# A gated cross-attention layer on one core: the second tile's input prepared during the weight folds, two input tiles turned earlier, and the second tile's probabilities turned in pieces

## The chip, the cores and the metric

The kernel runs on one core of one Trainium2 chip. The metric is the device time of one execution in microseconds. The version before the change took 1050.38 us (median of three runs, 1048.02 to 1050.64).

## The reference, cut to what matters

```python
q, k, v = split_heads(ln(x) @ Wq), split_heads(ctx @ Wk), split_heads(ctx @ Wv)   # 16 heads of 64
attn = softmax(q @ k.T * 64 ** -0.5)
x = x + tanh(g_xattn) * (merge_heads(attn @ v) @ Wo + bo)       # x is 4 x 2048 x 512, ctx is 4 x 77 x 384
idx = argmax(log_softmax(logits) + gumbel(u))                   # one of 8 weight matrices
x = x + tanh(g_ffn) * (ln(x) @ W[idx] + b[idx])
```

`ln` is a layer norm without weights, `merge_heads` puts the heads side by side.

## The kernel before, in words

**Folds.** The context is small (4 batches of 77 keys), so the program first folds weights into it. For each batch and head, Wq times the keys gives one matrix against which a normalized x is multiplied directly, and the values times Wo give one matrix by which the probabilities are multiplied. The folds are the visits of the list `VISITS`: 16 value visits (`VALUE`, PE line L1502), 32 key visits (`KEY`, PE L1510) and some others, on four pairs of PSUM banks in turn. Each fold is copied to float16 as a high part by ACT (L842 for values, L855 for keys) and as the remaining low part by DVE (L1098, L1109). For some folds ACT only stages a float32 copy (L840, L853), and POOL splits it (L681 and L683, L691 and L693). The next fold on a pair of banks waits until the fold four visits earlier has been taken. The value visits 13, 14 and 15 stand among the key visits 18 to 24; key visits 24 to 31 come last.

**Tiles.** Then x is worked off in 64 tiles of 128 rows, numbered 0 to 63; tile m is row block m // 4 of batch m % 4. A tile goes through these stages:

- `load_x` (SP, L497) brings tiles m+2 and m+3 at even m. `x_moments` (DVE, L1038) and `x_variance` (L1042), `x_scale` (POOL, L649 to L654), `x_normalized` and `x_high` (ACT, L792 and L799) and `x_low` (DVE, L450) make the normalized x as a high and a low float16 part in the stage `xs`. `turn_x` (SP, L487) transposes `xs` by a DMA.
- `scores` (PE, L1397, 36 matmuls) fills three of four PSUM banks. `maxima` (DVE, L1190, L1192), `exponentials` (ACT, 16 times L890), `softmax` (DVE, L1199, L1201), `probs_high` (ACT, L905, L907) and `probs_low` (DVE, L450) make the probabilities in two float16 parts in the one buffer `ps`. ACT's copy L990 fills its tail.
- SP turns `ps` into `pT` by a DMA transpose of 20 blocks (L589). There is one `pT`, so SP first waits for the semaphore `o_done`, which tells that the attention of the tile before is finished. For tiles 0 and 63 (`turned_early`) it goes in four pieces: 6 blocks of the high part and 6 of the low part (L582), which need the first 12 heads only, then 4 blocks (L586) and 4 blocks (L589).
- `attention` (PE, 27 matmuls of L1397 and two of L1625; in pieces L1608 to L1618) multiplies the turned probabilities by the folded values, and `attention_sum` (DVE, L1219) adds x.
- Two tiles later the feed-forward matrix is applied to a pair of tiles by seven products of half the size (Strassen's scheme; PE L1397 with 256 columns), with their stages turned by SP (L501, groups 0 to 3) and added by DVE (L1277). The seven weight combinations are made once, in the steps of tiles 0 to 2, by POOL (`weights_summed`), ACT (`weights_high`, L957) and DVE (`weights_low`, L1295) from a second load of the matrix (SP, L521).

**What sets the order.** Every engine runs `step` once a tile, and each engine's order within a step is written out by hand. The engines wait for each other by semaphores alone, and every engine, SP too, works in order: an instruction that waits holds all behind it. Step m computes scores of tile m and attention of tile m-1 on PE. DVE and ACT make the normalized x of tile m+1 in step m, and DVE takes the moments of tile m+2 there. Steps 0 to 5 are unrolled, steps 6 to 61 are seven turns of a loop of eight steps, and the last ones are unrolled again.

**Around the change.** Before the steps, tile 0 is made ready amid the folds: its moments at `(PROJECT, 3)`, its ACT part at `(VALUE, 2)` and `(REMAINDER, 3)`. Tile 1 has its moments at `(KEY, 24)`, and its ACT and DVE parts at the head of step 0, behind the last fold. On SP the transposes for tiles 0 and 1 stand behind waits for the folds:

```python
sp.wait_ge(v_folded, 4 * VALUES)
sp.dma_start(xr[:, 1, :], x[1, 0:P, :]).then_inc(x_loaded[1], 16)
sp.wait_ge(bo_set, 16 * 2 * B)
turn_x(0, 0)
sp.wait_ge(v_stage_lo, len(STAGED_VALUES))
sp.wait_ge(side_lo, 4 * KT)
sp.dma_start(wf_raw, ffn_w[...]).then_inc(wf_again, 16)
sp.wait_ge(k_stage_lo, key_staged_before(UNITS))
turn_x(0, 1)
```

`xr` has eight places for x tiles. Places 1 to 6 are under other data until the value folds are done; place 7 is free, apart from the turned x of tile 1, which stands there.

## Time and profile before

| | us |
|---|---|
| median of three runs | 1050.38 |
| the profiled execution's own time | 1049.61 |
| its span (first to last instruction) | 1047.8 |
| PE busy | 1029.6 (98% of the span) |
| DVE busy | 853.0 (81%) |
| ACT busy | 744.7 (71%) |
| POOL busy | 443.8 (42%) |
| PE's share of the chain that ended last | 91% |

PE's busy share counts every matmul from its start to its modelled end. The chain that ended last is followed back from the last instruction, at each step to what released it. Times in the tables of the trace count from the start of the span. The idle time before an instruction stands in brackets behind it, with what ended it.

### The profile page before, as it was taken

What the parts mean: (1) busy time and instruction counts of PE and PEld (TensorE: products, weight loads), DVE (VectorE), ACT (ScalarE), POOL (GpSimd) and SP (SyncE); (2) the same over time, 40 slices, a digit from 0 to 9 for tenths busy, and PEclk for the clock granted to TensorE, in tenths of its full rate; (3) what the DMA queues carried; (4) which work ended last, traced back from release to release, by engine and by line L of the source; (5) the groups of instructions that cost most, each with busy time, mean ns of one, the idle gap of its engine ahead of it and who ended that gap; (6) DMA issues with size and microseconds to landing.
All of it is one profiled execution on the core that took longest, in us unless ns stands there. A gap on an engine that the chain in (4) does not pass through costs nothing.

```text
span 1047.8 us, 21829 instructions
## 1 busy us (share of the span) xinstructions
PE 1029.6 (98%) x6065; PEld 588.2 (56%) x6065; DVE 853.0 (81%) x1802; ACT 744.7 (71%) x2712; POOL 443.8 (42%) x639
## 2 busy tenths in 40 slices
PE   8988899999999999999999999999999999999998
PEld 6634455555555555555555555555555555555555
DVE  4877988888888887888888887888888887888876
ACT  3588877767776777767776777767776777767762
POOL 1486443444333443444333443444333443444422
PEclk9999999999999999999999999999999999999999
DMA  8423476555666656655666656655666656655656
GB/s 307 99 37 98 94 127 141 126 112 119 135 138 138 136 126 133 134 114 115 133 139 138 136 125 134 134 115 114 133 139 138 137 123 135 136 114 114 133 113 141
DMA packets 383639, 135.02 MB, mean 129 GB/s; under 512 B 361728, under 2 KB 363316, under 8 KB 383540
## 3 DMA queue, kind: packets, MB, share of 16 engines
q1 hardware_dynamic: 383476, 134.09, 59.0%
q14 instruction: 84, 0.69, 0.2%
q8 instruction: 15, 0.25, 0.1%
q0 software_dynamic: 64, 0.00, 0.0%
HBM read 27.48 MB, written 16.78 MB: 42 GB/s over the span
## 4 chain that ended last, share of the span: by engine, by line
PE 91%; DVE 4%; DMA 2%; ACT 2%; issue 1%; SPq 0%; POOL 0%; DVEq 0%; ACTq 0%
PE banks L1397 82%; PE banks L1625 3%; PE banks L1427 1%; PE banks L1502 1%; PE banks L1438 1%; DMA work<-work 1%; ACT work L890 1%; PE banks L1510 1%; DMA fold_area<-in_L_xattn_Wv 1%; DVE work L450 1%; DVE vw_area L1098 1%; ACT vw_area L842 1%; PE banks L1491 1%; DVE fold_area L1109 0%; DVE work L1201 0%
## 5 line engine op out<-in xcount | busy, mean ns | idle before, releaser
L890 ACT ACTIVATE work<-banks,red,cst 128x77 f32<-128x77 f32 x1024 | 410.3, 431 | 83.9 <-DVE red L1192 83.4
L1397 PE MATMUL banks<-fold_area,work 128*128 128x456 f16 (+1 forms) x2304 | 405.4, 335 | 3.0 <-DMA work<-work 2.3
L1397 PE MATMUL banks<-vw_area,work 128*128 128x512 f16 x1674 | 373.1, 380 | 3.0 <-DMA work<-work 3.0
L1397 PEld LDWEIGHTS banks<-fold_area,work 128*128 128x128 f16 x2304 | 225.2, 98 | 171.6 <-DMA work<-work 3.1
L1397 PEld LDWEIGHTS banks<-vw_area,work 128*128 128x128 f16 x1674 | 164.0, 98 | 189.2 <-DMA work<-work 3.7
L450 DVE SCALAR_TENSOR_TENSOR work<-work 128x256 f16<-128x256 f32 (+3 forms) x443 | 240.9, 578 | 1.4 <-ACT work L799 0.6
L890 ACT ACTIVATION_READ_ACCUMULATOR work<-banks,red,cst 128x1 f32 x1024 | 224.8, 220 | 0.0
L1190 DVE TENSOR_REDUCE stats<-banks 128x6 f32<-128x462 f32 (+1 forms) x192 | 112.0, 583 | 103.9 <-PE banks L1397 103.7
L1397 PE MATMUL banks<-work 128*128 128x256 f16 x1302 | 162.4, 272 | 0.5 <-DVE work L1277 0.3
L1397 PEld LDWEIGHTS banks<-work 128*128 128x128 f16 x1302 | 126.8, 98 | 32.0 <-DVE work L1277 0.6
L734 POOL TENSOR_TENSOR stats<-stats,cst 128x1 f32<-128x1 f32 x64 | 12.5, 195 | 284.1 <-DVE stats L1226 284.1
L905 ACT ACTIVATE work<-work 128x768 f16<-128x768 f32 (+1 forms) x128 | 82.0, 640 | 58.6 <-DVE work L1201 58.6
L649 POOL TENSOR_TENSOR stats<-stats,cst 128x1 f32<-128x1 f32 x64 | 50.1, 783 | 169.4 <-DVE stats L1042 169.4
L792 ACT ACTIVATE work<-work,stats 128x512 f32<-128x512 f32 x64 | 52.1, 813 | 96.9 <-POOL stats L654 81.3
L1201 DVE TENSOR_TENSOR work<-work,cst 128x924 f32<-128x924 f32 (+1 forms) x128 | 113.5, 886 | 4.4
L1277 DVE SCALAR_TENSOR_TENSOR work<-banks,cst,work 128x256 f32<-128x256 f32 x217 | 97.9, 475 | 21.9 <-issue 18.2
L758 POOL TENSOR_TENSOR work<-work 128x512 f32<-128x512 f32 x64 | 95.9, 1499 | 43.0 <-DVE work L1235 33.5
L913 ACT ACTIVATE work<-work 128x512 f16<-128x512 f32 x123 | 71.1, 578 | 5.4 <-DMA work<-work 3.7
L1192 DVE TENSOR_SCALAR red<-stats,cst 128x6 f32<-128x6 f32 (+1 forms) x192 | 61.0, 318 | 6.8
L1219 DVE SCALAR_TENSOR_TENSOR work<-banks,cst,work 128x512 f32<-128x512 f32 x64 | 47.6, 744 | 6.8 <-PE banks L1625 3.6
L752 POOL TENSOR_TENSOR work<-work 128x256 f32<-128x256 f32 x31 | 45.2, 1459 | 2.4
L1222 DVE BATCH_NORM_STATS2 stats<-work 128x6 f32<-128x512 f32 x64 | 44.4, 694 | 2.2
(148 smaller groups left out, 819.4 us busy)
## 6 DMA issues: line engine op xcount, KB each, us to landing
work<-in_x SPq DMA_DIRECT2D x64, 256.0 KB, 2.8
out<-work SPq DMA_DIRECT2D x63, 256.0 KB, 2.2
work<-work SPq DMA_TRANSPOSE x253, 3.1
fold_area<-in_L_xattn_Wo SPq DMA_DIRECT2D x4, 512.0 KB, 9.6
work<-in_L_ffn_W SPq DMA_DIRECT2D x2, 1024.0 KB, 7.5
fold_area<-in_L_xattn_Wq SPq DMA_DIRECT2D x2, 1024.0 KB, 13.0
fold_area<-in_L_xattn_Wk SPq DMA_DIRECT2D x2, 768.0 KB, 12.4
fold_area<-in_L_xattn_Wv SPq DMA_DIRECT2D x2, 384.0 KB, 7.6
```

What stands on the lines that cost most here:

```text
L450: return nc.vector.scalar_tensor_tensor(out=lo, in0=value, scalar=scale, in1=hi, op0=ALU.mult, op1=ALU.subtract)
L649: nc.gpsimd.tensor_tensor(ve1, mv1[:, 1:2], eps, ALU.add).then_inc(ve1_ready, 1)
L758: nc.gpsimd.tensor_tensor(xr[:, m2, :], xr[:, m2, :], bias, ALU.add).then_inc(x2b_ready, 1)
L792: nc.scalar.activation(xn_place(o1, m1), xr[:, m1, :], ACT.Identity, bias=nm1, scale=rstd1).then_inc(xn_ready, 1)
L890: nc.scalar.activation(probs_of(place, place + 1), s_heads(m, k)[:, h - h0, :], ACT.Exp, bias=nmx[:, h:h + 1], scale=exp_scale, accum_out= ...
L905: nc.scalar.activation(by_core(ps[:, h0 * CORE:h1 * CORE]), values[:, :, 0:CORE], ACT.Copy, scale=2.0 ** PROB_BITS).then_inc(p_hi, 1)
L913: nc.scalar.activation(group_stage(g, last)[:, 0, :], value, ACT.Copy, scale=2.0 ** XN_BITS).then_inc(x2_hi, 1)
L1190: nc.vector.reduce_max(mx[:, h0:h1], s_heads(m, k), AX.X).then_inc(mx_ready, 1)
L1192: nc.vector.tensor_scalar(nmx[:, h0:h1], mx[:, h0:h1], nexp_scale, None, ALU.mult).then_inc(nmx_ready, 1)
L1201: nc.vector.tensor_tensor(values, values, factors.unsqueeze(2).to_broadcast([P, h1 - h0, J]), ALU.mult).then_inc(p_ready, 1)
L1277: nc.vector.scalar_tensor_tensor(out=half, in0=part, scalar=f_scale, in1=half, op0=ALU.mult, op1=ALU.add).then_inc(f_added, 1)
L1397: mm = nc.tensor.matmul(ps, lhs(l), rhs(r), start=first and n == 0, stop=last and n == 2, skip_group_check=onto)
```

## The change

1. **Tile 1's x during the folds.** A load of its own brings tile 1 into place 7 of `xr` (`x_second`) right behind tile 0's load. Its moments are taken at key visits 10 and 11, its scale at 14, its ACT parts at 20 and 21, and its low part at 22. The load into place 1 stays where it was, for `attention_sum`. SP turns tile 0 before it waits for the value folds, and tile 1 right behind that load, ahead of the second load of the feed-forward matrix.
2. **Tiles 2 and 3.** DVE makes their low part after two of the three maxima of steps 1 and 2, not after all three.
3. **Every even step on SP.** `turn_x` now stands ahead of the two loads of x, where it stood behind them.
4. **Tile 1's probabilities** are turned in the four pieces, and multiplied so. The load of the bias moves behind them.
5. Two semaphores of start-up constants become one.

```diff
--- before.py
+++ after.py
@@ -142,6 +142,7 @@
         bias = c.take(D)
         assert c.at == 16592
         ident = bias[:, 0:P]
+        x_second = xr[:, RING - 1, :]
         xT_second = xr[:, RING - 1, :].bitcast(F16).rearrange("p (s k n) -> p s k n", s=2, k=KT)
         pT_last = fold_area[:, 0:KEYS // 2].bitcast(F16).rearrange("p (c n) -> p c n", n=P)
 
@@ -322,7 +324,7 @@
         EARLY = BANKS[1][1] * CORE // P
 
         def turned_early(o, m):
-            return is_tile(o, m, 0, NT - 1)
+            return is_tile(o, m, 0, 1, NT - 1)
 
         def heads_of(piece):
             return BANKS[piece[0]][0], BANKS[piece[1] - 1][1]
@@ -473,6 +475,7 @@
                 rows = slice(n * KT // 2, (n + 1) * KT // 2)
                 sp.dma_start(wq_raw[:, rows, :], wq.rearrange("(k p) n -> p k n", p=P)[:, rows, :]).then_inc(wq_loaded[n], 16)
             sp.dma_start(xr[:, 0, :], x[0, 0:P, :]).then_inc(x_loaded[0], 16)
+            sp.dma_start(x_second, x[1, 0:P, :]).then_inc(x_second_loaded, 16)
 
             def due(semaphore, count):
 
@@ -512,15 +515,15 @@
                 for s in range(2):
                     sp.dma_start(vw_side[TAIL + TH:TAIL + TH + 1, :, b, 2 * s + 1, :],
                                  bo_split[0:1, s, :].rearrange("p (t n) -> p t n", t=KT)).then_inc(bo_set, 16)
+            sp.wait_ge(bo_set, 16 * 2 * B)
+            turn_x(0, 0)
             sp.wait_ge(v_folded, 4 * VALUES)
             sp.dma_start(xr[:, 1, :], x[1, 0:P, :]).then_inc(x_loaded[1], 16)
-            sp.wait_ge(bo_set, 16 * 2 * B)
-            turn_x(0, 0)
+            turn_x(0, 1)
             sp.wait_ge(v_stage_lo, len(STAGED_VALUES))
             sp.wait_ge(side_lo, 4 * KT)
             sp.dma_start(wf_raw, ffn_w[bass.ds(op, 1), :, :].rearrange("o (k p) n -> p (o k) n", p=P)).then_inc(wf_again, 16)
             sp.wait_ge(k_stage_lo, key_staged_before(UNITS))
-            turn_x(0, 1)
 
             def step(o, m):
                 o1, m1 = tile(o, m, 1)
@@ -536,12 +539,12 @@
                         if positive(*pair, 2):
                             due(f_done, nth_pair(*pair, PRODUCTS))
                         turn_group(2)
+                    if valid(o1) and not is_tile(o, m, 0):
+                        turn_x(o1, m1)
                     for lag in (2, 3):
                         ol, ml = tile(o, m, lag)
                         if valid(ol):
                             load_x(ol, ml)
-                    if valid(o1) and not is_tile(o, m, 0):
-                        turn_x(o1, m1)
                     if is_tile(o, m, NT):
                         turn_lone(NT - 2)
                     if valid(pair[0]) and paired(*pair):
@@ -571,10 +574,8 @@
                     early = turned_early(o, m)
                     if not positive(o, m, 1):
                         sp.wait_ge(pad_zeroed, 2)
-                    elif not early:
+                    elif not early or is_tile(o, m, 1):
                         due(o_done, nth(o, m))
-                    if is_tile(o, m, 1):
-                        sp.dma_start(bias, ffn_b[bass.ds(op, 1), :].to_broadcast([P, D])).then_inc(bias_loaded, 16)
                     if early:
 
                         for s, half_ready in enumerate((p_hi, p_lo)):
@@ -587,6 +588,8 @@
                     due(p_lo, nth(o, m, 4) + 4)
                     start = NC + EARLY if early else 0
                     sp.dma_start_transpose(turned[:, start:, :], ps[:, start * P:]).then_inc(pT_turned, 16)
+                    if is_tile(o, m, 1):
+                        sp.dma_start(bias, ffn_b[bass.ds(op, 1), :].to_broadcast([P, D])).then_inc(bias_loaded, 16)
                 if is_tile(o, m, NT):
                     store_pair(*tile(o, m, -6))
                 if is_tile(o, m, NT + 1):
@@ -701,7 +704,7 @@
                     key_split(n)
                 if (kind, n) == (REMAINDER, 1):
                     x_scale(0, 0)
-                if (kind, n) == (KEY, 24):
+                if (kind, n) == (KEY, 14):
                     x_scale(0, 1)
 
             pool.wait_ge(a_done, 2 * UNITS)
@@ -789,7 +792,7 @@
                 if not is_tile(o1, m1, 0, 1):
                     act.wait_ge(xT_turned, nth(o1, m1, 16))
                     act.wait_ge(p_lo, nth(o1, m1, 4) - 4)
-                nc.scalar.activation(xn_place(o1, m1), xr[:, m1, :], ACT.Identity, bias=nm1, scale=rstd1).then_inc(xn_ready, 1)
+                nc.scalar.activation(xn_place(o1, m1), x_second if is_tile(o1, m1, 1) else xr[:, m1, :], ACT.Identity, bias=nm1, scale=rstd1).then_inc(xn_ready, 1)
 
             def x_high(o1, m1):
 
@@ -876,6 +879,10 @@
                     x_normalized(0, 0)
                 if (kind, n) == (REMAINDER, 3):
                     x_high(0, 0)
+                if (kind, n) == (KEY, 20):
+                    x_normalized(0, 1)
+                if (kind, n) == (KEY, 21):
+                    x_high(0, 1)
             act.wait_ge(exp_scale_ready, 2)
 
             def exponentials(o, m, k):
@@ -898,9 +905,9 @@
                     act.wait_ge(pad_zeroed, 2)
                 elif n == 0:
                     act.wait_ge(pT_turned, nth(o, m, 16))
-                    if is_tile(o, m, 1):
+                    if is_tile(o, m, 1, 2):
                         for part_turned in pT_parts:
-                            act.wait_ge(part_turned, 16)
+                            act.wait_ge(part_turned, 16 * number(o, m))
                 values = by_head(probs_of(h0, h1))
                 nc.scalar.activation(by_core(ps[:, h0 * CORE:h1 * CORE]), values[:, :, 0:CORE], ACT.Copy,
                                      scale=2.0 ** PROB_BITS).then_inc(p_hi, 1)
@@ -962,7 +969,7 @@
                 grouped = valid(pair[0]) and paired(*pair)
                 if is_tile(o, m, NT + 1):
                     lone_high(NT - 1)
-                if valid(o1):
+                if valid(o1) and not is_tile(o, m, 0):
                     x_normalized(o1, m1)
                     x_high(o1, m1)
                 if grouped:
@@ -1034,8 +1041,11 @@
 
             def x_moments(o1, m1):
 
-                dve.wait_ge(x_loaded[m1], o1 * 16 + 16)
-                nc.vector.bn_stats(bn1, xr[:, m1, :]).then_inc(x_stats, 1)
+                if is_tile(o1, m1, 1):
+                    dve.wait_ge(x_second_loaded, 16)
+                else:
+                    dve.wait_ge(x_loaded[m1], o1 * 16 + 16)
+                nc.vector.bn_stats(bn1, x_second if is_tile(o1, m1, 1) else xr[:, m1, :]).then_inc(x_stats, 1)
 
             def x_variance():
 
@@ -1175,11 +1185,13 @@
                     x_low(0, 0)
                 if (kind, n) == (KEY, 12):
                     scales()
-                if (kind, n) == (KEY, 24):
+                if (kind, n) == (KEY, 10):
                     x_moments(0, 1)
-                if (kind, n) == (KEY, 25):
+                if (kind, n) == (KEY, 11):
                     dve.wait_ge(x_stats, 2)
                     x_variance()
+                if (kind, n) == (KEY, 22):
+                    x_low(0, 1)
 
             NB = len(BANKS)
 
@@ -1216,6 +1228,8 @@
                 dve.wait_ge(o_done, nth(o, m) + 1)
                 if not positive(o, m, 1):
                     dve.wait_ge(o_scale_ready, 2)
+                if is_tile(o, m, 1):
+                    dve.wait_ge(x_loaded[1], 16)
                 nc.vector.scalar_tensor_tensor(out=xr[:, m, :], in0=o_ps, scalar=o_scale, in1=xr[:, m, :],
                                                op0=ALU.mult, op1=ALU.add).then_inc(x2_ready, 1)
                 dve.wait_ge(x2_ready, nth(o, m) + 1)
@@ -1346,8 +1360,6 @@
                     added(*begun, 3)
                 if valid(o2):
                     dve.wait_ge(x2_stats, nth(o2, m2) + 1)
-                if is_tile(o, m, 0):
-                    x_low(o1, m1)
                 if valid(o):
                     maxima(o, m, 0)
                 if grouped:
@@ -1356,11 +1368,13 @@
                     x2_variance(o2, m2)
                 if valid(o):
                     maxima(o, m, 1)
+                if is_tile(o, m, 1, 2):
+                    x_low(o1, m1)
                 if valid(o2):
                     x2_normalized(o2, m2)
                 if valid(o):
                     maxima(o, m, 2)
-                if valid(o1) and not is_tile(o, m, 0):
+                if valid(o1) and not is_tile(o, m, 0, 1, 2):
                     x_low(o1, m1)
                 if is_tile(o, m, 1):
                     weights_low(AS_LOADED, 0)
@@ -1584,7 +1598,7 @@
             def attention(o, m):
 
                 b, turned, early = m % B, probs_place(o, m), turned_early(o, m)
-                turns = 16 if is_tile(o, m, 0) else 32
+                turns = 16 if is_tile(o, m, 0) else 32 if is_tile(o, m, 1) else 48
                 if early:
                     pe.wait_ge(pT_parts[0], turns)
                 else:```

The order of the instructions on ACT, at the end of the folds and the head of step 0, was this (`vw_area` and `fold_area` hold the folded values and keys; L840 and L853 are staged copies, L792 and L799 tile 1's normalized x and its high part, L957 the weights):

```order
L842 CAST vw_area<-banks 128x1024
L855 CAST fold_area<-banks 128x4x76x2
L840 COPY work<-banks 128x1024
L855 CAST fold_area<-banks 128x4x76x2
L842 CAST vw_area<-banks 128x1024
L855 CAST fold_area<-banks 128x4x76x2
L853 COPY work<-banks 128x608
L855 CAST fold_area<-banks 128x4x76x2 x6
L853 COPY work<-banks 128x608
L855 CAST fold_area<-banks 128x4x76x2
L792 ACTIVATE work<-work,stats 128x512
L799 ACTIVATE work<-work 128x512
```

With the change it is this (lines are three higher):

```order
L845 CAST vw_area<-banks 128x1024
L858 CAST fold_area<-banks 128x4x76x2
L795 ACTIVATE work<-work,stats 128x512
L843 COPY work<-banks 128x1024
L858 CAST fold_area<-banks 128x4x76x2
L802 ACTIVATE work<-work 128x512
L845 CAST vw_area<-banks 128x1024
L858 CAST fold_area<-banks 128x4x76x2
L856 COPY work<-banks 128x608
L858 CAST fold_area<-banks 128x4x76x2 x6
L856 COPY work<-banks 128x608
L858 CAST fold_area<-banks 128x4x76x2
```

The two instructions of tile 1 moved from behind the last key fold to either side of value visit 14, ahead of 11 of its copies.

SP's queue from the bias rows to tile 1's probabilities was this (`[waits ...]` names the semaphores waited for):

```order
L513 DMA vw_area<-work 1x4x128 x7
L516 DMA work<-in_x 128x512 [waits v_folded]
L487 DMA_TRANSPOSE work<-work 128x8x128 [waits bo_set,x_lo]
L521 DMA work<-in_L_ffn_W 128x4x512 [waits side_lo,v_stage_lo]
L487 DMA_TRANSPOSE work<-work 128x8x128 [waits k_stage_lo,x_lo]
L497 DMA work<-in_x 128x512 x2
```

It is now:

```order
L516 DMA vw_area<-work 1x4x128 x7
L490 DMA_TRANSPOSE work<-work 128x8x128 [waits bo_set,x_lo]
L521 DMA work<-in_x 128x512 [waits v_folded]
L490 DMA_TRANSPOSE work<-work 128x8x128 [waits x_lo]
L525 DMA work<-in_L_ffn_W 128x4x512 [waits side_lo,v_stage_lo]
L500 DMA work<-in_x 128x512 [waits k_stage_lo]
```

Both transposes of x (L487, now L490) moved ahead by one transfer each; the matrix's second load stands behind the second.

SP's queue of an even step, number 4, was this (L501 turns groups of the feed-forward, L589 the probabilities):

```order
L501 DMA_TRANSPOSE work<-work 128x8x128 [waits x2_lo]
L497 DMA work<-in_x 128x512
L497 DMA work<-in_x 128x512 [waits xT_turned]
L487 DMA_TRANSPOSE work<-work 128x8x128 [waits x_lo,s_done]
L501 DMA_TRANSPOSE work<-work 128x4x128 [waits x2_lo]
L589 DMA_TRANSPOSE work<-work 128x20x128 [waits o_done,p_tail,p_lo]
```

And now:

```order
L504 DMA_TRANSPOSE work<-work 128x8x128 [waits x2_lo]
L490 DMA_TRANSPOSE work<-work 128x8x128 [waits x_lo,s_done]
L500 DMA work<-in_x 128x512
L500 DMA work<-in_x 128x512 [waits xT_turned]
L504 DMA_TRANSPOSE work<-work 128x4x128 [waits x2_lo]
L590 DMA_TRANSPOSE work<-work 128x20x128 [waits o_done,p_tail,p_lo]
```

The two loads stand behind the waits of the transpose of x.

## Rows read from the trace of the kernel before

**Rows 1.** Waits of PE from 91 to 143 us: total, times, longest.

```profile
PE banks L1397 <- DMA work<-work: 5.3, 4, 2.6
```

**Rows 2.** PE in order of time: start us, duration us, what, idle before.

```profile
91.56 6.33 PE L1397 MATMUL banks<-fold_area,work 128*128 128x456 f16 x36 [0.77 <-ACT work L853]
99.36 6.34 PE L1397 MATMUL banks<-fold_area,work 128*128 128x456 f16 x36 [1.47 <-DMA work<-work]
...
121.75 7.69 PE L1397 MATMUL banks<-vw_area,work 128*128 128x512 f16 x27 [2.64 <-DMA work<-work]
...
136.42 6.00 PE L1397 MATMUL banks<-vw_area,work 128*128 128x512 f16 x27 [0.38 <-DMA work<-work]
```

**Rows 3.** Busy time by stretch; PEclk is the granted share of TensorE's clock.

```profile
121.75:125.10 3.35, 3.35 (x9) 1.21 (x10) 3.21 (x7) 3.35 (x17) 0.00 (x0) 0.52 0.76 212
```

**Rows 4.** The chain that ended last, 129 to 137 us: start us, us, what.

```profile
129.44 0.45 PE banks L1625 x2
...
130.56 5.81 DMA work<-work
```

**Rows 5.** ACT in order of time, the last folds and the head of step 0.

```profile
80.77 0.70 ACT L855 CAST fold_area<-banks 128x608 f16<-128x608 f32 x1
81.59 1.01 ACT L840 COPY work<-banks 128x1024 f32<-128x1024 f32 x1
...
83.42 1.01 ACT L842 CAST vw_area<-banks 128x1024 f16<-128x1024 f32 x1 [0.21 <-PE banks L1502]
...
91.43 0.82 ACT L792 ACTIVATE work<-work,stats 128x512 f32<-128x512 f32 x1
92.28 0.63 ACT L799 ACTIVATE work<-work 128x512 f16<-128x512 f32 x1
92.81 1.32 ACT L957 ACTIVATE work<-work,red 128x512 f16<-128x512 f32 x2
...
95.16 0.42 ACT L890 ACTIVATE work<-banks,red,cst 128x77 f32<-128x77 f32 x1 [1.03 <-DVE red L1192]
```

**Rows 6.** DVE in order of time.

```profile
69.46 1.23 DVE L1098 TENSOR_TENSOR vw_area<-banks,vw_area 128x1024 f16<-128x1024 f32 x1 [1.17 <-ACT vw_area L842]
...
87.06 0.68 DVE L1038 BATCH_NORM_STATS2 stats<-work 128x6 f32<-128x512 f32 x1
...
92.94 1.37 DVE L450 SCALAR_TENSOR_TENSOR work<-work 128x512 f16<-128x512 f32 x1 [0.58 <-ACT work L799]
...
127.74 1.67 DVE L450 SCALAR_TENSOR_TENSOR work<-work 128x768 f16<-128x768 f32 x4
```

**Rows 7.** POOL in order of time.

```profile
85.40 2.13 POOL L683 TENSOR_TENSOR vw_area<-work,vw_area 128x1024 f16<-128x1024 f32 x1
...
92.10 1.65 POOL L693 TENSOR_TENSOR fold_area<-work,fold_area 128x608 f16<-128x608 f32 x1
```

**Rows 8.** SP's issues in order of time.

```profile
87.56 0.41 SPq L521 DMA_DIRECT2D work<-in_L_ffn_W  x1
94.41 1.25 SPq L487 DMA_TRANSPOSE work<-work  x1
```

**Rows 9.** Line L521 from 87 to 88 us.

```profile
DMA to landing us min/median/max: 5.1/5.1/5.1
```

**Rows 10.** SP's issues in step 8 and step 14.

```profile
209.96 1.23 SPq L487 DMA_TRANSPOSE work<-work  x1
...
305.56 3.01 SPq L589 DMA_TRANSPOSE work<-work  x1
```

**Rows 11.** Line L497, the two loads of x from 207 to 209 us.

```profile
DMA to landing us min/median/max: 2.6/2.7/2.7
```

**Rows 12.** DVE in step 8.

```profile
212.27 0.69 DVE L1038 BATCH_NORM_STATS2 stats<-work 128x6 f32<-128x512 f32 x1
```

**Rows 13.** Line L589, the 58 transposes of probabilities from 150 to 1000 us.

```profile
DMA to landing us min/median/max: 4.9/4.9/6.5
```

**Rows 14.** PE, attention of tile 14.

```profile
312.48 0.81 PE L1397 MATMUL banks<-vw_area,work 128*128 128x512 f16 x3
```

13 lines of the change are left out of this document (7 added, 6 removed).

## The prediction

> **What bounds the kernel now.** I read the page first: PE is busy 98% of the span and 91% of the chain that ended last, so there is little to win, and only where PE stands still. The waits of PE show where: from 91 to 143 us it waits 5.3 us for transposes, four times [rows 1], and after that hardly at all until the tail. PE in order of time gives the places [rows 2]: 1.47 us before the scores of tile 1, 2.64 before the attention of tile 1, 0.38 before the attention of tile 2, which leaves 0.80 for the scores of tile 2. There is a second loss behind the longest wait: the 27 matmuls at 121.75 take 7.69 us, and the same 27 at 136.42 take 6.00 [rows 2]. The granted clock in the first 3.35 us of the slow ones is 0.52 [rows 3], mostly the lower of the two levels (1.2 instead of 2.4 GHz). The engine had been idle for 2.64 us before it, while the wait of 1.47 us left the clock alone. So all that this change can reach is 5.3 + 1.69 = 7.0 us, plus what it does to the folds.
>
> The question is then what sets the last of these waits, because behind it PE runs through: the total moves by as much as the end of tile 2's attention moves. The chain says that its transpose at 130.56 was released by PE itself, by the end of tile 1's attention (129.44 + 0.45) [rows 4], since the buffer is shared. But DVE's low parts of tile 2's probabilities end only at 127.74 + 1.67 = 129.41 [rows 6]. If PE comes earlier, the transpose can start at 129.5 at the earliest, 1.1 us sooner, unless DVE and ACT come earlier too. That is the step on which I rest.
>
> **The change part by part.** I count against the profiled execution (1049.61 us, 0.77 below the median of the runs, 1050.38).
>
> *Tile 1's moments.* DVE's 0.68 us at key visits 10 and 11 fall into an idle 1.17 us before 69.46 [rows 6]: nothing. POOL's scale lies ahead of a split that has no one waiting; it moves POOL by under 1 us and is made up by its removal at visit 25. The load of its own (256 KB behind tile 0's) has over 40 us: nothing.
>
> *ACT amid the folds.* Its two instructions take 0.82 + 0.63 = 1.45 us [rows 5]. Idle time that can take them is 81.59 - (80.77 + 0.70) = 0.12 and 0.21 us [rows 5], so the copy of value visit 15, at 83.42, comes up to 1.1 us later, and all key visits behind it are in its tow.
>
> *DVE amid the folds.* The low part stands, within one key fold, where the moments' 0.68 us stood at 87.06 [rows 6]. It is the same tile of work, but in the trace it took 1.37 us at 92.94 [rows 6], while POOL's subtraction ran from 92.10 to 93.75 [rows 7]; it ended 0.56 us after that. In its new place POOL's longer subtraction (2.13 us at 85.40 before [rows 7]) is running. Bounds: equal to the moments (0) and 1.37 - 0.68 = 0.7 more; I take 0.7, since that row is of the same instruction beside the same kind of work. The Trainium skill (SBUF — State Buffer, "SBUF: two separate sides") says that a VectorE operation with two SBUF inputs and a GpSimd operation that reads SBUF lock a port pair for a whole instruction and block each other fully. The trace agrees (0.56 us after POOL's end). By that rule alone the worst case is 2.13 + 0.56 = 2.7 us, and the sum would be 1.3 us higher than mine; the sum goes by the row.
>
> Together: ACT's delay of up to 1.1 partly hides in DVE's waits for ACT, the 0.7 adds up. The scores of tile 0, released by the last staged copy at 91.56 [rows 2], start 0.3 (all but a remainder hidden) to 1.8 us (both in full) later; I take 1.3.
>
> *Start of tile 0's exponentials*, now at 95.16 [rows 5]. Two things hold them. Through the scores: 1.3 later, less 0.3 that DVE's low part of tile 1 had cost there (it ended at 94.31 [rows 6], the first bank, 12 of the 36 matmuls, at about 91.56 + 2.4), so 96.2. Through SP: the second load of the matrix, issued at 87.56 [rows 8], now stands behind the transpose of tile 1, which waits for the low part (87.06 + 1.37 = 88.4) and takes 1.25 us to issue [rows 8], so it goes out at 89.8. It lands 5.1 us later [rows 9], plus some 0.3 for sharing the DMA engines with that transpose: 95.2. ACT's two weight copies, 1.32 us [rows 5], wait for it and stand ahead of the exponentials: 96.5. The later one counts: **the chain of tile 0 starts 1.4 us later** (0.3 to 2.2), although tile 1's x is ready early. What the folds gain PE, namely the wait of 1.47 us, only turns up again as a wait of about 1.7 us before tile 0's attention, whose first pieces come 1.4 us later.
>
> *From there to tile 2.* ACT and DVE are back to back from these exponentials to DVE's end at 129.41, and nothing in between is removed. Tile 2's and 3's low parts only change places with a maximum (0 to 0.3, if POOL's sums hit them; 0). So tile 2's probabilities are ready at 129.41 + 1.4 = 130.8.
>
> *Tile 1's pieces.* SP now issues the first 6 blocks while the last heads' low parts are still made, about 2 us before the whole transpose could have gone, and PE needs the rest only 2.6 us after its start. The attention of tile 1 follows the scores of tile 2 without a wait: 2.64 and the 1.69 us of slow clock are gone there. PE then comes to tile 2's attention at about 92.85 + 4 x 6.2 (scores) + 2 x 6.4 (attention) + 1.7 (wait) = 132.2.
>
> *Tile 2's attention* is not turned in pieces. Issued at 130.9, landed 5.81 us later [rows 4], it starts at 136.75 instead of 136.42: **+0.3**. Landing in 4.9 us, the usual value [rows 13], would make it -0.6. PE has then stood still for some 4.5 us, longer than the 2.64 us that were followed by the low clock, so I let the slow stretch come back here, once: the 27 matmuls take 7.69 again, **+1.7**. With no slow stretch the bound is 0.
>
> *Loads behind `turn_x`.* In each even step the two loads now wait for the transpose of x. In step 8 it is issued at 209.96 [rows 10], so the load goes at about 211.3 and lands at 213.9 with 2.6 to 2.7 us [rows 11]. DVE takes that tile's moments at 212.27 [rows 12]: a new wait of 1.65 us on DVE, with the last softmax and the low parts queued behind it. PE waits for these through the transpose. In the tightest even step, 14 (the first of each turn of the loop), it is issued at 305.56 [rows 10], lands after 4.9 [rows 13], and PE takes it at 312.48 [rows 14]: 2.0 us of slack, of which 0.4 are left. So it costs nothing as long as landings stay at 4.9; the cover is that slack.
>
> Sum: +0.3 + 1.7 + 0 = +2.0 us on 1049.61, or 1050.38 + 2.0 = **1052.4** for the median. That is 0.19%; about 0.3% (3.15 us) is what a measurement of this kernel can tell from no change, so it reads as no difference.
>
> **The rivals.** *A, the wait moves and the clock holds.* The low clock followed one idle stretch in this part of the trace, and one case is thin ground. With it gone, or with a landing of 4.9 us, the sum is -0.6 to +0.6; with the chain only 0.3 late it is -1.7: 1048.7 to 1051.0, say 1050.4.
>
> *B, slower: the loop's slack breaks.* One of the 58 transposes took 6.5 us to land [rows 13], so landings do vary. If the loads' 1.65 us exceed what the first even step of each loop turn has left, PE stops there: with half a microsecond in each of seven turns, 3.5 us on top of 2.0, so 1055.9. It decides from 0.4 us of lateness on. Against it: the median landing is also the least, 4.9 us [rows 13].
>
> *C, faster: PE's gain is kept.* If the chain of waits is right that PE's own end released tile 2's transpose, and ACT and DVE come earlier with it, 5.3 + 1.69 less 0.4 for tile 2 is won: 1050.38 - 6.6 = 1043.8. Against it: the 129.41 of rows 6 would have to become 125 or so, and the folds' end moves the other way.
>
> **How the numbers follow.** Forecast 0.62, A 0.14, B 0.16, C 0.08. The forecast's own bounds run from 1050.5 (chain 0.4 late, clock low) to 1053.2 (chain 2.2 late). For the range I go down over A's middle and up to most of B: 1049.0 to 1055.5; outside are C, the top of B and the bottom of A. Faster by over 0.3% is C (0.08); slower by over 0.3% is B and a little of the forecast's top (0.18); the rest is 0.74.
>
> **What would show it.** Right if: PE has no wait between the scores of tiles 0 and 1, waits 1 to 2.5 us before tile 0's attention, none before tile 1's and 4 to 5 us before tile 2's; 7.7 us instead of 6.0 in tile 2's attention and 6.0 in tile 1's; L957's first copies start at about 95 us; DVE waits 1.5 to 1.8 us for a load in every even step. Wrong if tile 2's transpose is issued before 129.5 us, if the exponentials of tile 0 start at 95.2 or before, or if PE waits in the loop.

## The result, and the profile after

| | before | after |
|---|---|---|
| median of 20 runs each, on one chip | 1048.10 us | 1052.56 us |
| ratio, 95% interval | | 1.0044 [1.0032, 1.0056] |
| the profiled execution, its own time / span | 1049.61 / 1047.8 us | 1058.05 / 1056.2 us |

The change costs 0.44%, some 4.6 us: slower by more than the 0.3% that can be told from no change. The forecast was 1052.4, +2.0 us on a median of 1050.38. That the time came within 0.2 us of the forecast is luck: the kernel before ran at 1048.1 this time, 2.3 us faster than the median that I had counted from, and of the difference the forecast had less than half. The interval leaves out two disturbed runs of after (2793.52 and 3848.48 us); the others lie between 1048.36 and 1058.05, and the profiled one is the slowest of them. Its rows show mechanisms, and their sizes have to be averaged over runs.

PE of after in order of time, to be read against [rows 2]. L1411 is what L1397 was, L1622 begins an attention in pieces.

```profile
93.99 12.50 PE L1411 MATMUL banks<-fold_area,work 128*128 128x456 f16 x72 [0.77 <-ACT work L856]
108.02 2.76 PE L1622 MATMUL banks<-vw_area,work 128*128 128x512 f16 x12 [1.53 <-DMA work<-work]
...
120.46 2.75 PE L1622 MATMUL banks<-vw_area,work 128*128 128x512 f16 x12
...
128.47 6.34 PE L1411 MATMUL banks<-fold_area,work 128*128 128x456 f16 x36 [1.59 <-DMA work<-work]
138.06 8.94 PE L1411 MATMUL banks<-vw_area,work 128*128 128x512 f16 x27 [3.25 <-DMA work<-work]
```

The 72 matmuls at 93.99 are the scores of tiles 0 and 1 without a wait. Tile 0's attention waits 1.53 us, tile 1's not at all, the scores of tile 3 wait 1.59, tile 2's attention 3.25, and its 27 matmuls take 8.94 us. The windows of PE there (us, PE busy, PEclk, DMA share, GB/s), against [rows 3]:

```profile
138.06:143.00 4.94, 4.94 (x12) 0.50 0.35 66
143.00:146.80 3.80, 3.80 (x16) 0.86 0.37 69
```

The clock stood at its lower level (1.2 of 2.4 GHz) for 6.8 us in all (0.85 us of it still in the pause), twice as long as in before.

ACT of after amid the last folds and at the head of step 0, against [rows 5]:

```profile
82.49 0.83 ACT L795 ACTIVATE work<-work,stats 128x512 f32<-128x512 f32 x1
84.67 0.66 ACT L802 ACTIVATE work<-work 128x512 f16<-128x512 f32 x1
85.20 1.03 ACT L845 CAST vw_area<-banks 128x1024 f16<-128x1024 f32 x1
96.48 1.33 ACT L964 ACTIVATE work<-work,red 128x512 f16<-128x512 f32 x2 [2.53 <-DMA work<-in_L_ffn_W]
97.72 0.40 ACT L897 ACTIVATE work<-banks,red,cst 128x77 f32<-128x77 f32 x1
```

DVE's low part of tile 1, against [rows 6], and POOL's subtraction beside it, against [rows 7]:

```profile
88.10 1.37 DVE L452 SCALAR_TENSOR_TENSOR work<-work 128x512 f16<-128x512 f32 x1
```

```profile
86.80 2.13 POOL L686 TENSOR_TENSOR vw_area<-work,vw_area 128x1024 f16<-128x1024 f32 x1
```

DVE's instruction took 1.37 us again and ended 89.47 - 88.93 = 0.54 us after POOL's, as it had ended 0.56 after it in before; the matrix's load landed at 96.38, and ACT's weight copies and the exponentials stood behind it. The chain that ended last (start us, us, what) holds the transfers, against [rows 4, 9]:

```profile
91.03 5.35 DMA work<-in_L_ffn_W
...
96.48 1.33 ACT work L964 x2
...
132.55 5.46 DMA work<-work
...
138.06 2.31 PE banks L1411 x5
```

The start of the program differs between executions. So I count from the start of tile 0's moments on DVE (42.45 us in before, 43.60 in after). From there:

| start of | before | after | difference | forecast |
|---|---|---|---|---|
| scores of tile 0 | 49.11 | 50.39 | +1.28 | +1.3 |
| exponentials of tile 0 | 52.71 | 54.12 | +1.41 | +1.4 |
| attention of tile 2 | 93.97 | 94.46 | +0.49 | +0.3 |
| attention of tile 4 | 122.77 | 126.21 | +3.44 | +2.0 |
| attention of tile 61 | 961.80 | 969.03 | +7.23 | +2.0 |

The first three lines came as forecast. The fourth is 1.4 us above its forecast, nearly all of it in tile 2's attention, which took 8.94 us and not 7.69. The last line holds 3.79 us that are lost between tile 4 and tile 61, where I had put nothing. The waits from 150 to 1010 us show where (total, times, longest), DVE's and then PE's:

```profile
DVE stats L1048 <- DMA work<-in_x: 53.5, 29, 3.6
```

```profile
PE banks L1411 <- DMA work<-work: 2.5, 3, 1.0
```

29 waits of DVE for a load, 1.84 us each, were forecast (1.65). In before DVE waits for no load in this stretch and PE for no transpose. One of PE's three waits, and how it came about, told by the chain that ended last:

```profile
319.21 6.00 PE L1411 MATMUL banks<-vw_area,work 128*128 128x512 f16 x27 [0.85 <-DMA work<-work]
```

```profile
306.87 1.23 SPq L490
...
308.41 2.52 DMA work<-in_x
...
310.95 0.71 DVE stats L1048
...
313.31 0.78 DVE work L452 x3
...
314.19 4.90 DMA work<-work
...
319.21 2.98 PE banks L1411 x13
```

The transpose of x goes first, then the load, then DVE's moments, the last softmax and low parts, then the transpose of tile 14's probabilities, then PE. All transfers have their usual length here, and PE still waited 0.85 us. The slack of 2.0 us that I read from [rows 10, 13, 14] was more than gone: the transpose was issued 319.21 - 0.85 - 314.19 = 4.17 us before PE was ready for it, where it had been 6.92 in before. That is 2.75 us later, not the 1.65 that I had counted.

One thing in the waits of before bears on why the first even step of a turn is the tightest, and my account had left it out. Six times, at the start of a turn, DVE stands still for some 3 us, for which the profile shows no releaser. What it does in that time is not shown. The line gives the total, the times and the longest:

```profile
DVE work L1277 <- issue: 18.2, 6, 3.1
```

### The profile page after: what moved, and what is told of

It reads as the page before. It is cut to its first block, busy times and chain, and to the rows that moved or that the text cites. A ratio compares the mean times of both kernels' runs of the same rounds, so it can differ in the third digit from the quotient of the medians.

```text
span 1056.2 us, 21836 instructions
## 1 busy us (share of the span) xinstructions
PE 1033.6 (98%) x6065; PEld 589.3 (56%) x6065; DVE 854.1 (81%) x1802; ACT 740.0 (70%) x2712; POOL 443.5 (42%) x639
## 4 chain that ended last, share of the span: by engine, by line
PE 75%; DVE 8%; DMA 5%; issue 4%; ACT 3%; POOL 2%; SPq 2%; DVEq 0%; ACTq 0%; POOLq 0%
PE banks L1411 67%; DVE work L452 3%; PE banks L1639 2%; ACT work L897 2%; DMA work<-in_x 2%; DMA work<-work 1%; PE banks L1441 1%; PE banks L1452 1%; PE banks L1516 1%; SPq L490 1%; DVE stats L1202 1%; DVE stats L1048 1%; ACT vw_area L845 1%; DMA fold_area<-in_ctx 1%; DVE vw_area L1108 1%
## 5 line engine op out<-in xcount | busy, mean ns | idle before, releaser
L897 ACT ACTIVATE work<-banks,red,cst 128x77 f32<-128x77 f32 x1024 | 409.7, 428 | 35.8 <-DVE red L1204 35.8
L1411 PE MATMUL banks<-fold_area,work 128*128 128x456 f16 (+1 forms) x2304 | 405.2, 335 | 2.4 <-DMA work<-work 1.6
L1411 PE MATMUL banks<-vw_area,work 128*128 128x512 f16 x1647 | 368.4, 381 | 5.8 <-DMA work<-work 5.8
L1411 PEld LDWEIGHTS banks<-fold_area,work 128*128 128x128 f16 x2304 | 225.3, 98 | 170.6 <-DMA work<-work 2.1
L1411 PEld LDWEIGHTS banks<-vw_area,work 128*128 128x128 f16 x1647 | 161.1, 98 | 191.2 <-issue 8.0
L452 DVE SCALAR_TENSOR_TENSOR work<-work 128x256 f16<-128x256 f32 (+3 forms) x443 | 243.8, 585 | 2.6 <-ACT work L920 1.8
L897 ACT ACTIVATION_READ_ACCUMULATOR work<-banks,red,cst 128x1 f32 x1024 | 222.9, 218 | 0.0
L1411 PE MATMUL banks<-work 128*128 128x256 f16 x1302 | 162.4, 272 | 0.9 <-DVE work L1291 0.5
L1411 PEld LDWEIGHTS banks<-work 128*128 128x128 f16 x1302 | 126.6, 98 | 32.5 <-issue 1.2
L795 ACT ACTIVATE work<-work,stats 128x512 f32<-128x512 f32 x64 | 52.1, 813 | 97.1 <-POOL stats L657 81.6
L1213 DVE TENSOR_TENSOR work<-work,cst 128x924 f32<-128x924 f32 (+1 forms) x128 | 108.1, 844 | 7.8 <-DVE cst L1211 3.9
L1048 DVE BATCH_NORM_STATS2 stats<-work 128x6 f32<-128x512 f32 x64 | 44.0, 687 | 54.3 <-DMA work<-in_x 54.3
L1204 DVE TENSOR_SCALAR red<-stats,cst 128x6 f32<-128x6 f32 (+1 forms) x192 | 65.6, 341 | 6.8
L1236 DVE BATCH_NORM_STATS2 stats<-work 128x6 f32<-128x512 f32 x64 | 44.5, 695 | 2.2
```

The costliest lines, as they stand in the source:

```text
L452: return nc.vector.scalar_tensor_tensor(out=lo, in0=value, scalar=scale, in1=hi, op0=ALU.mult, op1=ALU.subtract)
L795: nc.scalar.activation(xn_place(o1, m1), x_second if is_tile(o1, m1, 1) else xr[:, m1, :], ACT.Identity, bias=nm1, scale=rstd1).then_inc(x ...
L897: nc.scalar.activation(probs_of(place, place + 1), s_heads(m, k)[:, h - h0, :], ACT.Exp, bias=nmx[:, h:h + 1], scale=exp_scale, accum_out= ...
L1048: nc.vector.bn_stats(bn1, x_second if is_tile(o1, m1, 1) else xr[:, m1, :]).then_inc(x_stats, 1)
L1204: nc.vector.tensor_scalar(nmx[:, h0:h1], mx[:, h0:h1], nexp_scale, None, ALU.mult).then_inc(nmx_ready, 1)
L1213: nc.vector.tensor_tensor(values, values, factors.unsqueeze(2).to_broadcast([P, h1 - h0, J]), ALU.mult).then_inc(p_ready, 1)
```

## The experiments

Theory P: what the change lost is lost before the loop, in tile 2's attention, by the pause and its low clock. Theory L: the loads behind `turn_x` stop PE in the loop. Every kernel was compared with the kernel before on the same chip (23 to 35 runs of it, median 1047.88 to 1048.38); the times are medians of 12 runs, except where a number stands. Differences between kernels measured on different chips are differences of such ratios, and their intervals are wider, some 0.2% to each side. "Part 1" is tile 1's x made ready amid the folds, "part 2" the low parts of tiles 2 and 3 ahead of a maximum, "part 3" the loads behind `turn_x`, "part 4" tile 1's probabilities in pieces. Part 2 was tried by itself in no run. "Theory V" in the later expectations is L with its reason: the later loads leave PE no slack in the loop, and those that land late stop it.

The first four kernels undo or do one part. Their expectations were written with the first profile in view, in which 2.9 of 4.6 us seemed to be the low clock.

**Loads ahead again.** The changed kernel with

```diff
-                    if valid(o1) and not is_tile(o, m, 0):
-                        turn_x(o1, m1)
                     for lag in (2, 3): ...
+                    if valid(o1) and not is_tile(o, m, 0):
+                        turn_x(o1, m1)
```

> The changed kernel with its third part undone: in even steps SP issues the two loads of x ahead of the transpose of x again. Theory (the loads make DVE wait in every even step, 29 waits of together 53.5 us, and the delay is not worked off before the first even step of each loop turn, where PE waits): DVE's waits for loads vanish, PE has no wait after 150 us, and 2.5 to 4 us come back, 1049 to 1050 us, ratio to the kernel before 1.001 to 1.002. Tile 2's attention still starts late and at the low clock. Rival (the loop's waits of PE come from elsewhere, such as slow transfers or instruction loading): PE still waits in the loop, about 1052.5 us, ratio 1.004.

Measured: 1049.34 us, ratio 1.0016 [1.0005, 1.0026]. PE does not wait in the loop. Before it:

```profile
127.93 6.34 PE L1411 MATMUL banks<-fold_area,work 128*128 128x456 f16 x36 [3.45 <-DMA work<-work]
135.29 6.00 PE L1411 MATMUL banks<-vw_area,work 128*128 128x512 f16 x27 [1.01 <-DMA work<-work]
```

The pause has moved ahead of the scores of tile 3, whose transpose now stands behind two loads and the bias. It is longer than the 3.25 us of after, and the clock stayed up. So a pause of this length does not bring the low clock each time. Theory L has its range here; that tile 2's attention would still run at the low clock did not come.

**Loads behind, alone.** The kernel before with part 3 (the diff above, reversed).

> The kernel before with the third part alone: the two loads behind the transpose of x. Theory: DVE waits about 1.7 us in each even step, PE loses 2 to 4 us in the loop, about 1051 us, ratio 1.002 to 1.004, and the stretch up to 150 us is as before. My forecast's own reading (the slack of 2.0 us takes 1.65 us without a loss): ratio 1.000. Rival (the turn ahead of the loads is worth something by itself): below 1.000.

Measured: 1047.74 us, ratio 1.0000 [0.9989, 1.0011]. DVE waits 54.0 us for loads, 29 times, as in after, and PE stops once in the loop, for 0.44 us; between tiles 4 and 61 0.95 us are lost. That is the forecast's own reading, and theory L's 1051 is out for this kernel. By itself the part costs nothing that can be measured, though taking it from the changed kernel gains 0.3%.

**Pieces, alone.** The kernel before with tile 1 in `turned_early`, the bias load behind its transposes, and the counts of `pT_parts` raised.

> The kernel before with the fourth part alone: tile 1's probabilities turned in pieces. Theory (tile 2's probabilities are bound by ACT and DVE at 129.4, so PE's gain turns into one wait of 3 to 4 us before tile 2's attention, and the low clock moves there): attention of tile 1 starts without a wait and takes 6.0 us, that of tile 2 starts at most 1.1 us sooner and takes 7.7 to 8.9 us; in all 0 to +1.8 us, ratio 1.000 to 1.002. Rival (PE's gain of 2.64 + 1.69 us is kept): 4 us faster, ratio 0.996.

Measured: 1048.07 us (11 runs), ratio 1.0003 [0.9992, 1.0014].

```profile
124.97 8.03 PE L1397 MATMUL banks<-fold_area,work 128*128 128x456 f16 x36 [2.03 <-DMA work<-work]
```

Tile 1's attention no longer waits. PE waits 2.03 us for tile 3's x in its place (I had looked for the wait at tile 2's attention), and here the low clock came behind 2.03 us. What the pieces gain at one transpose is mostly given back at the next, and the rival's 4 us are out.

**Early x, alone.** The kernel before with part 1 (moments at key visits 10 and 11, ACT's part at 20 and 21, DVE's at 22, its own load, both transposes of x issued earlier).

> The kernel before with the first part alone: tile 1's x made ready amid the folds. Theory (the folds and the second load of the matrix put tile 0's exponentials 1.4 us later, and every chain behind them): no wait before tile 1's scores, one of about 1.5 us before tile 0's attention, tile 1's and tile 2's attention 1.4 us later than before, +1.4 us, ratio 1.001 to 1.002. Rival (the early x saves PE's wait of 1.47 us): ratio 0.9985.

Measured: 1048.82 us, ratio 1.0001 [0.9990, 1.0011]. In the trace, tile 0's exponentials start 1.6 us and tile 2's attention 1.2 us later than in before, and the runs do not show that: their interval reaches from -1.0 to +1.1 us, so a median of 12 runs hardly carries a term of this size. The delay itself repeats from trace to trace: counted from tile 0's moments, its scores start at 50.37 to 50.41 us in all nine traces with part 1 and at 49.10 to 49.15 in all five without.

**Pairs of parts.** Each of the three parts alone costs nothing that the runs can tell, and all together cost 0.44%. The next two kernels leave something out: the change without the pieces (parts 1, 2 and 3), then parts 3 and 4 on the kernel before.

> The change without the pieces of tile 1's probabilities: early x, low parts ahead of a maximum, loads behind the transpose of x. Theory P (what the change lost is the long low-clock stretch in tile 2's attention, 6.8 us instead of 3.4, 2.9 us in all): the pause falls before tile 1's attention again (1.5 to 2.6 us), the low stretch is 3.4 us as in the kernel before, tile 2's attention starts 1.2 us later as with the early x alone, so about 1049.5 (+1.2). Theory L (the loads behind the transpose cost only where the chain is already late, as it is with the early x): PE stands still at the first even step of several turns of the loop, 0.4 to 1 us each, 2.5 to 3.8 us in all, so 1051.5 to 1053.

> The kernel before with loads behind and the pieces of tile 1, without the early x. Theory P: PE does not wait before the scores of tile 3 (it waited 2.03 us there with the pieces alone, the transpose standing behind loads), but stands still 2.5 to 4 us before tile 2's attention; if the low clock follows for 6 to 7 us, as in the changed kernel, the time is 1050 to 1051; if for 3.4 us or not at all, 1047.5 to 1048.5. Theory L: no early x, so the chain is on time, the loop has under 1 us of waits in all and the time is 1048 +- 0.6.

Measured: 1049.88 us, 1.0024 [1.0009, 1.0039], and 1050.07 us, 1.0023 [1.0010, 1.0037]. The first was between the two theories: the pause before tile 1's attention (3.56 us, low clock 3.4 us) and one wait of 1.0 us in the loop, 1.50 us lost between tiles 4 and 61. In the second, PE before the loop:

```profile
134.09 8.63 PE L1397 MATMUL banks<-vw_area,work 128*128 128x512 f16 x27 [3.82 <-DMA work<-work]
```

The low clock lasted 6.8 us, 0.08 us was lost in the loop, and the time is what P gives for that. Beside part 4, part 3 thus costs 0.20% (1.0023 against 1.0003, give or take 0.18%), beside parts 1 and 2 it is 0.23% with part 2 in it (1.0024 against 1.0001); both are barely clear of nothing. Part 2 shows no delay of its own: with it and part 3, tile 4's attention starts 123.56 us after tile 0's moments, with part 1 alone 123.99. Neither theory is enough.

**The pause filled.** The changed kernel with 13 matmuls of filler, which tile 2's attention overwrites; the wait for the transposed probabilities stands behind them:

```diff
+                if is_tile(o, m, 2):
+                    for n in range(13):
+                        nc.tensor.matmul(o_ps, vw[:, b, 0, 0, 0:P], vw[:, b, 0, 1, :], start=True, stop=True)
```

> The changed kernel with 13 matmuls of 128x512 (2.9 us) that only fill PE's wait before tile 2's attention; the attention's first product overwrites what they wrote. Theory P: the pause brings the low clock, so filled it goes: tile 2's attention takes 6.0 to 6.2 us instead of 8.94, starts at most 0.3 us later, and the time falls by 2.5 to 2.9 us, to 1049.7. Rival N (the low stretch has nothing to do with the pause, since 3.45 us of pause were not followed by it in the kernel with the loads ahead): tile 2's attention still takes 7.7 to 8.9 us and the time stays at 1052.5. Rival M (the low clock follows the pause in part of the executions only): the time falls by 1 to 1.5 us in the median.

Measured: 1051.83 us (9 runs), ratio 1.0039 [1.0022, 1.0056].

```profile
132.57 2.97 PE L1616 MATMUL banks<-vw_area 128*128 128x512 f16 x13
135.99 6.00 PE L1411 MATMUL banks<-vw_area,work 128*128 128x512 f16 x27 [0.45 <-DMA work<-work]
```

The pause is gone, the 27 matmuls take 6.00 us, and the ratio falls by 0.0005, or 0.5 us, where P wanted 2.5 or more. None of the three named outcomes is met by the median, but the difference is uncertain by some 2.2 us, so this kernel alone decides little; 5 of its 9 runs still have some low clock. What speaks against P as a full account is the granted clock of each execution. Of 90 runs of the kernel before, 29 have no low clock at all (mean 1046.9 us) and 41 a mean clock of 0.998, about one stretch of 3.4 us (mean 1048.2). Of 24 runs of the changed kernel 3 have none (mean 1050.4) and 16 have 0.998 (mean 1052.9). At equal clock it is 3.5 to 4.7 us slower (6.4 us at 0.998 on the one chip that has both in these counts), so most of the lost time is not the low clock.

**Two tiles in pieces.** A candidate: tile 2 in pieces too, the loads behind `turn_x` in step 2 only, the bias loaded in step 0.

> The changed kernel with three edits: tile 2's probabilities are turned in pieces too, the loads stand behind the transpose of x in step 2 only, and the bias is loaded in step 0. Theory: PE's waits before the scores of tile 3 fall from 1.6 to about 0.5 us and before tile 2's attention from 3.25 to under 1 us, no low clock follows, tile 2's attention ends 5 to 7 us earlier than in the changed kernel and 2 to 4 us earlier than in the kernel before; half of that is given back as a wait before the scores of tile 4. Time 1045 to 1047. Rival (ACT and DVE set the pace, PE's gain is given back in the steps behind): 1048 +- 0.6.

Measured: 1047.46 us, ratio 0.9991 [0.9979, 1.0003]; spread 1046.65 to 1049.85. It is 5.1 us better than the changed kernel's median, and the same as before. So the rival is met, and not the 1045 to 1047 of the theory. Nine of its 12 runs have no low clock; its longest wait of PE from the scores on is 1.5 us.

**Loads behind in step 2 only.** That edit by itself, on the changed kernel:

```diff
-                    if valid(o1) and not is_tile(o, m, 0):
+                    if valid(o1) and not is_tile(o, m, 0) and is_tile(o, m, 2):
                         turn_x(o1, m1)
                     for lag in (2, 3): ...
+                    if valid(o1) and not is_tile(o, m, 0) and not is_tile(o, m, 2):
+                        turn_x(o1, m1)
```

> The changed kernel with the loads behind the transpose of x in step 2 only, ahead of it from step 4 on, as in the kernel before. Theory V (in the loop the later loads leave PE no slack, and loads that land late, 4.2 to 4.6 us in place of 2.8, now stop it: 1.3 us on average, between 0.1 and 3.8 in the five traces that have the loads behind): no PE wait in the loop, DVE does not wait for x there, and the time falls by 1 to 3 us against the changed kernel, to 1050 to 1051.5, with a narrower spread. Rival P (what the change lost is lost before the loop, in tile 2's wait and its low clock): still 1052.5.

Measured: 1050.18 us, ratio 1.0025 [1.0013, 1.0036]. Neither DVE nor PE waits for a transfer in the loop. The steps before it are those of the changed kernel, to 0.1 us, up to tile 2's attention:

```profile
126.19 6.34 PE L1413 MATMUL banks<-fold_area,work 128*128 128x456 f16 x36 [1.65 <-DMA work<-work]
135.74 6.00 PE L1413 MATMUL banks<-vw_area,work 128*128 128x512 f16 x27 [3.20 <-DMA work<-work]
```

Its loop is as fast as before's in the trace (839.02 against 839.03 us from tile 4's to tile 61's attention). So 2.6 us of the change are lost before the loop (1.4 to 3.8 by the interval), and what the loads cost in the loop is the rest.

**Loads last.** The changed kernel with the two loads behind the group of 4 blocks as well.

> The changed kernel with the two loads of an even step one more transfer further back, behind the group of 4 blocks. Theory V: DVE's wait for x grows from 1.8 us per even step by at least the 1.3 us that the group's issue takes, to over 3 us; the first even step of each of the seven turns has nothing left and PE stops there for about 1.3 us, and in others too, 7 to 12 us in all: 1059 to 1064. Rival P: the loop has slack yet, DVE's wait grows and PE's does not, 1053 +- 1.

Measured: 1127.20 us (5 runs), ratio 1.0753 [1.0735, 1.0770]. Both theories missed by 60 us or more; only the direction is L's. The waits from 150 to 1010 us, DVE's and PE's:

```profile
DVE stats L1048 <- DMA work<-in_x: 114.5, 27, 4.5
```

```profile
PE banks L1411 <- DMA work<-work: 44.4, 27, 1.8
PE banks L1411 <- DVE work L1291: 15.1, 12, 1.5
```

DVE's wait grew from 1.8 to 4.2 us per even step, by 2.4. I had counted one PE stop per turn of the loop and some more; PE stopped 27 times for a transpose, about once per even step, and 12 times more for DVE's sums of the feed-forward. The 71.7 us lost between tiles 4 and 61 are 2.6 us in each of 28 even steps, about the growth of DVE's wait. So, as far as one kernel shows it, the first 1.8 us use up about all the slack, and what comes on top is paid in full.

**The change again**, for a second profile.

> The changed kernel itself, for a second profile and more times. Theory V: PE's waits in the loop differ from the 3.8 us of the first profile (0.1 to 1.5 us, as in the other kernels with the loads behind); tile 0's and tile 2's milestones before the loop repeat within 0.2 us but for the low clock, which comes for 0, 3.4 or 6.8 us; median 1051.5 to 1052.5. Rival P: low clock of 6.8 us in tile 2's attention again.

Measured: 1054.67 us (6 runs), ratio 1.0058 [1.0042, 1.0074]. The starts up to tile 2's attention repeat within 0.2 us. The low clock lasted 3.4 us this time:

```profile
134.54 7.69 PE L1411 MATMUL banks<-vw_area,work 128*128 128x512 f16 x27 [3.25 <-DMA work<-work]
```

Tile 4's attention starts 124.80 us after tile 0's moments, 2.03 later than in before. That is the +0.3 and +1.7 of the forecast in the one trace that has the one low stretch it assumed. Between tiles 4 and 61 5.85 us were lost, more than the 3.79 of the first profile and not the 0.1 to 1.5 that I expected; the median too lies above the 1051.5 to 1052.5 that I gave. PE's waits there, but for a fourth of 0.95 us in tile 46's attention:

```profile
313.71 6.00 PE L1411 MATMUL banks<-vw_area,work 128*128 128x512 f16 x27 [1.07 <-DMA work<-work]
432.98 6.00 PE L1411 MATMUL banks<-vw_area,work 128*128 128x512 f16 x27 [1.13 <-DMA work<-work]
670.12 6.00 PE L1411 MATMUL banks<-vw_area,work 128*128 128x512 f16 x27 [0.91 <-DMA work<-work]
```

These are tiles 14, 22 and 38, and with tile 46 each is the first even step of a turn.

**Two tiles in pieces, x late.** The last candidate leaves part 1 out: the kernel before with

```diff
-            return is_tile(o, m, 0, NT - 1)
+            return is_tile(o, m, 0, 1, 2, NT - 1)
...
-                    if is_tile(o, m, 1):
+                    if is_tile(o, m, 0):
                         sp.dma_start(bias, ...)
```

and the loads behind `turn_x` in step 2 only, the low parts of tiles 2 and 3 ahead of a maximum, and the counts that follow.

> The kernel before (tile 1's x made ready in step 0) with tiles 1 and 2 turned in pieces, the low parts of tiles 2 and 3 ahead of a maximum, the loads behind the transpose in step 2 only and the bias loaded in step 0. Theory: it is the kernel with both in pieces less the 1.3 us by which the early x delays tile 0, so 1046.0 to 1047.0 and no loop waits. Rival (the early x pays for its delay there, by the wait before tile 1's scores that it removes): 1047.5 to 1048.5.

Measured: 1045.60 us, ratio 0.9983 [0.9974, 0.9991], all runs within 1045.12 to 1047.59. It beats the changed kernel clearly and the kernel before by 0.17%; the theory's 1046.0 to 1047.0 was a little too slow. PE from the scores of tile 1 on:

```profile
97.37 6.34 PE L1401 MATMUL banks<-fold_area,work 128*128 128x456 f16 x36 [1.38 <-DMA work<-work]
...
110.84 6.34 PE L1401 MATMUL banks<-fold_area,work 128*128 128x456 f16 x36 [0.86 <-DMA work<-work]
...
123.53 6.34 PE L1401 MATMUL banks<-fold_area,work 128*128 128x456 f16 x36
129.71 2.75 PE L1612 MATMUL banks<-vw_area,work 128*128 128x512 f16 x12
...
136.92 6.34 PE L1401 MATMUL banks<-fold_area,work 128*128 128x456 f16 x36 [0.78 <-DMA work<-work]
```

Tile 2's attention (129.71) starts 89.20 us after tile 0's moments, 4.8 us earlier than in before; 2.6 of that are given back by tile 4's attention, most of it in two waits of step 4 (0.78 and 1.44 us), and 2.2 are kept. Of these, 1.69 are the low clock that before's profile has and this one has not. No pause reaches 1.5 us, and 9 of 12 runs have no low clock, against 29 of 90. Among the runs without low clock on this chip it is 1.2 us faster (1045.6 against 1046.7 in the mean), so part of the gain is the rarer low clock and part is not. That the early x is what the other kernel loses by is argued, not shown: 0.9983 and 0.9991 have intervals that overlap.

## Why the prediction was right or wrong

**Right, by the rows of the profiles.** ACT and DVE amid the folds: scores of tile 0 +1.28 us (1.3). The matrix's load behind the second `turn_x`: issued at 91.03, landed after 5.35, exponentials +1.41 (1.4). DVE's low part took 1.37 us beside POOL, 0.7 more than the moments. The rule of the Trainium skill that I had weighed there (SBUF — State Buffer, "SBUF: two separate sides") agrees again in that the instruction ended just behind POOL's; its worst case, 2.7 us, did not come. Tile 1's attention without a wait. Tile 2's attention +0.49 (0.3). Rival C is out: the transpose went at 132.55, or 131.40 in before's count of time, far behind 129.5. Two errors half cancel in the last term. The transpose landed after 5.46 us and not 5.81, and it was issued 0.5 us later than I had it, for a reason that my account had at nothing, the bias load behind tile 1's transposes. ACT waited for it in the middle of tile 2's exponentials:

```profile
127.51 0.72 ACT L985 ACTIVATE work<-work,cst 128x512 f32<-128x512 f32 x1 [0.53 <-DMA work<-in_L_ffn_b]
```

**The pauses.** I had "some 4.5 us before it" in one place; it was 1.59 + 3.25 = 4.84, split, since the scores of tile 3 wait for their own transpose. So the sign of 4 to 5 us before tile 2's attention failed.

**The clock, +1.7.** In the profiles it was 6.8, 3.4 and 0 us of low clock behind the same pause of 3.2 us (after, its repeat, the kernel with the loads behind in step 2 only). The term is a chance, not a length. The change seems to make it likelier: 21 of 24 runs have some, 61 of 90 before, and over all kernels with a pause of 3 us or more it is 63 of 77 (with 6 of 12 in the fifth, whose pause is 3.56 us). The mean clock of the changed kernel's runs and before's, 0.9979 against 0.9983, makes 0.5 us of it; most of the low clock was there before too. With one low stretch in both kernels, the +0.3 and +1.7 stand for a chain that has lost its gain at tile 1 and pays the same clock at tile 2, and the repeat's +2.03 us at tile 4 bears that out. The whole stretch before the loop measures +2.6 us [+1.4 to +3.8] (the ninth kernel), and I had +2.0. Rival A's sum has a slip: with a landing of 4.9 us and the low clock, its own terms give -0.6 + 1.7 = +1.1, not +0.6 at most.

**The step that failed** is "Loads behind `turn_x`", which I put at 0: "So it costs nothing as long as landings stay at 4.9". It costs the difference between the changed kernel and the ninth: 2.0 us, give or take 1.7 (1.0044 against 1.0025), and in the repeat, on the ninth kernel's chip, 3.5, give or take 2.1. By the sign that I had named, PE waiting in the loop, this step is wrong. Rival B had the place and the size, 3.5 us on top of 2.0, and I gave it 0.16. Its condition, that the 1.65 us exceed what the first even step of a turn has left, is what came about; the reason that it gave for it, a transpose that lands late, is not, for in the chain above PE stopped with a landing of 4.90. What I left out was that a step can be late already: of the 2.75 us by which tile 14's transpose moved, the wait of its own step is 1.71, and the rest came from the steps before, which I had taken to be worked off in between (that they are not is read from this trace and was not tried by itself). With 0.4 of slack left over there was no cover for it. I had read the slack at one step of one trace, and had not asked what happens once it is used up; in the tenth kernel 2.4 us more of wait cost 2.6 us in each of 28 even steps.

**Still open.** The loop's loss was 0.95, 1.50, 0.08 and 0.40 us in four other traces with the loads where the change has them, and 3.79 and 5.85 in the two of the changed kernel itself; with the loads ahead it was at most 0.01 in six other traces, counted from before. The 0.40 is the kernel with the filler, whose loop is the changed kernel's but for the order of two waits of PE. Why the changed kernel loses more there than the others with this loop is not shown, nor how much of it is chance between executions. In five of these six traces a load near 211 to 216 us landed after 4.1 to 4.7 us, where with the loads ahead none took over 3.2 us in the loop; but most of PE's waits lie elsewhere.

## What to carry to other kernels

When a transfer is put behind a wait in a queue, compare the whole chain from that wait to the bound engine with its slack in the tightest step, with what earlier steps leave behind added to it. Here a slack of 2.0 us against 1.65 us of new wait was enough with that part alone and not enough in the changed kernel; once the slack was used up, in the tenth kernel, the cost was paid in every even step. A pause of the bound engine that is removed at one transpose comes back at the next one unless that is made ready earlier too; here only turning two tiles in pieces, with the bias and the loads out of the way, kept a gain, and it is 0.17%. Where executions differ by more than the effect, count from a common event behind the start-up, and size a term by many runs of kernels that differ in it alone; a ratio from 12 runs is good to some 1.1 to 1.6 us here.

## What the runs showed of the hardware

- The low clock behind a pause of TensorE is not a rule of this kernel but a draw: 2.03 and 2.64 us were followed by 3.4 us of it, 3.25 us by 6.8 in one execution and 3.4 in another, 3.56 and 3.82 us by 3.4 and 6.8, and 3.20 and 3.45 us by none. Two kernels whose pauses there stay at or under 1.5 us had none in 9 of 12 runs each.
- One low stretch of 3.4 us costs about 1.3 us in the time (1048.2 against 1046.9 over 70 runs of the kernel before, and 0.9 to 2.0 us on the three chips taken singly), beside 1.69 us that the matmuls of before's profile lose.
- With the loads of 256 KB issued by SP behind the transpose of x, one or two of them near 211 to 216 us landed after 4.1 to 4.7 us in five of six traces; issued ahead of it, none took over 3.2 us from 150 us on. The order is not the whole of it: with the loads still further back (the tenth kernel) none took over 3.1 us, and before the loop loads that went ahead took up to 4.1 us in before and 5.4 in the first kernel.
